# Zero-weight matmuls in the gaps of a recurrent scan on TensorE

## The reference

```python
def step(h, xt):                       # one step of the scan, h is [8,128]
    cell_inputs = jnp.concatenate([xt, h], axis=-1)
    m = cell_inputs @ weight + bias
    g_act = m[:, :units]
    c_act = m[:, units:]
    c = jnp.tanh(c_act)
    g = jax.nn.sigmoid(g_act + 1.0)
    h_new = g * h + (1.0 - g) * c
    return (h_new, h_new)
...
x = x + _L0_cond_ref(x, cond_1024, L0_cond_weight, L0_cond_bias)
x = x + _L1_cond_ref(x, cond_1024[:, None, :], ...)   # the block: norms, q/k/v, 16 heads of 8, FF 512
```

## Time and profile before

| | |
|---|---|
| median of 3 runs | 536.1 us (534.92 to 538.26) |
| the profiled execution's span | 539.5 us |
| TensorE matmul busy | 419.0 us (78%) |
| TensorE weight loads busy | 267.0 us (49%) |
| VectorE busy | 317.5 us (59%) |
| ScalarE busy | 225.6 us (42%) |
| GpSimd busy | 155.8 us (29%) |
| mean granted TensorE clock, by the profile | 0.826 |

### The profile page before, as it was taken

One profiled execution on the slowest core, in us unless ns is written; L12 is line 12 of the kernel. 1 busy time (PEld: TensorE's weight loads), 2 busy tenths in 40 slices (PEclk: granted clock), 3 DMA queues, 4 the chain that ended last, 5 costly groups with the idle time before them and its releaser, 6 DMA issues.

```text
span 539.5 us, 14126 instructions
## 1 busy us (share of the span) xinstructions
PE 419.0 (78%) x5187; PEld 267.0 (49%) x5187; DVE 317.5 (59%) x1827; ACT 225.6 (42%) x996; POOL 155.8 (29%) x343
## 2 busy tenths in 40 slices
PE   2988897876669685899998995869999999974040
PEld 1647655555457474566575653532333354353040
DVE  5444445758857678757577644660116356688864
ACT  1233223243432342454544554365465645734230
POOL 5000000224701218201417105420021423558542
PEclk9999999999999999999999999755565555565555
DMA  6109000000000000000000000000000000000000
GB/s 172 35 11 213 18 1 2 2 2 2 2 2 2 2 1 2 3 2 2 2 2 2 2 2 2 2 1 2 1 1 1 2 2 1 16 6 13 7 20 19
DMA packets 8010, 7.88 MB, mean 15 GB/s; under 512 B 1203, under 2 KB 6589, under 8 KB 7942
## 3 DMA queue, kind: packets, MB, share of 16 engines
q1 hardware_dynamic: 7846, 6.72, 5.4%
q0 software_dynamic: 96, 0.26, 0.2%
HBM read 5.91 MB, written 1.07 MB: 13 GB/s over the span
## 4 chain that ended last, share of the span: by engine, by line
PE 61%; DVE 19%; ACT 10%; POOL 5%; issue 4%; DMA 1%; SPq 0%; DVEq 0%; POOLq 0%; ACTq 0%
PE zb L686 17%; PE zb L836 7%; PE tb L637 5%; PE zb L858 5%; PE tb L779 5%; PE firsts L858 5%; DVE prod_hi L1223 4%; ACT state L993 3%; PE zb L665 3%; PE firsts L836 3%; DVE prod_lo L1229 2%; ACT state L996 2%; PE zb L671 2%; PE firsts L686 1%; PE firsts L637 1%
## 5 line engine op out<-in xcount | busy, mean ns | idle before, releaser
L686 PE MATMUL zb<-prod_hi,whh 128*128 128x8 f16 x1920 | 90.9, 171 | 42.4 <-DVE prod_hi L1223 41.3
L686 PEld LDWEIGHTS zb<-prod_hi,whh 128*128 128x128 f16 x1920 | 73.6, 106 | 96.1 <-DVE prod_hi L1223 88.2
L993 ACT ACTIVATE state<-zb 128x8 f32<-128x8 f32 x240 | 42.4, 177 | 170.4 <-PE zb L686 170.4
L1223 DVE SCALAR_TENSOR_TENSOR prod_hi<-state 128x16 f16<-128x16 f32 x255 | 47.4, 186 | 99.3 <-ACT state L996 95.1
L686 PE MATMUL zb<-prod_lo,whh 128*128 128x8 f16 x960 | 63.7, 172 | 3.0 <-DVE prod_lo L1229 1.2
L1105 ACT ACTIVATE pr<-zb 128x256 f32<-128x256 f32 x96 | 42.9, 455 | 40.9 <-PE zb L858 39.9
L1229 DVE TENSOR_TENSOR prod_lo<-prod,prod_hi 128x16 f16<-128x16 f32 x255 | 50.3, 197 | 8.7
L501 POOL TENSOR_TENSOR stat<-mv 128x4 f32<-128x4 f32 x8 | 1.6, 201 | 167.0 <-DVE mv L1310 160.0
L686 PEld LDWEIGHTS zb<-prod_lo,whh 128*128 128x128 f16 x960 | 44.4, 107 | 6.6 <-DVE prod_lo L1229 3.8
L836 PE MATMUL zb<-pr,V 128*18 128x256 f32 (+1 forms) x512 | 46.6, 457 | 0.7 <-ACT pr L1105 0.7
L858 PE MATMUL zb<-QT,KT 32*128 32x256 f16 (+1 forms) x320 | 43.4, 264 | 1.4 <-ACT pr L1105 1.4
(11 more groups left out here) (288 smaller groups left out, 744.4 us busy)
## 6 DMA issues: line engine op xcount, KB each, us to landing
mod<-ada_rows SPq DMA_DIRECT2D x4, 768.0 KB, 12.4
resid<-in_x_dram SPq DMA_DIRECT2D x6, 128.0 KB, 3.6
out_dram<-state SPq DMA_DIRECT2D x8, 64.0 KB, 2.1
out_dram<-early SPq DMA_DIRECT2D x8, 64.0 KB, 2.1
yy<-in_L_cond_w_ada_dram SPq DMA_DIRECT2D x1, 384.0 KB
early<-in_L_cond_weight_dram SPq DMA_DIRECT2D x2, 128.0 KB
resid<-in_x_dram POOLq DMA_DIRECT2D x2, 128.0 KB, 3.5
w<-in_L_cond_w_f_dram SPq DMA_DIRECT2D x1, 256.0 KB
```

Of the source, the lines that this page charges most:

```text
L686: i = pe.matmul(z_bank(t, k)[:, NB * (t % CH):NB * (t % CH) + NB], whh[:, half, p, k, :], src[:, NB * p:NB * p + NB], start=False, stop=Fa ...
L993: act.activation(r[:, 24:32], z_bank(t, 1)[:, k:k + NB], ACT.Tanh, scale=-1.0 / ZS)
L1223: dve.scalar_tensor_tensor(prod_hi[:, :], r[:, 16:32], 1.0, r[:, 0:16], ALU.add, ALU.mult).then_inc(hi_ready, 1)
```

## The change

TensorE gets matmuls whose weights are a tile of zeros (`zeros`, f16, set by VectorE at its program's start) and whose moving operand is the identity read repeatedly. They add zero to bank `zb[:, .., 0, :]` of the chunk that the scan is not in. Ten of them, of 512 columns each, stand between the transposes of `x` and `first_x_part`. In the scan a last worker, `filler`, puts some into each tick up to 249: 512 + 512 + 256 columns if no background worker put anything on TensorE since its last turn, and else 512 columns. To know that, the matmuls and transposes of the kernel are counted (`issued`).

```diff
+KEEP = STEPS - 6
+FULL, SHORT = (512, 512, 256), (512,)
...
+        zeros = sb("zeros", [P, P], F16)
...
+            def matmul(dst, left, right, **flags):
+                issued[0] += 1
+                return pe.matmul(dst, left, right, **flags)
+
+            def keep_busy(bank, sizes, first=False):
+
+                for n in sizes:
+                    pe.matmul(bank[:, 0:n], zeros[:, :], view(identh[:, 0:1], [0, n // P], [1, P]),
+                              start=first, stop=True, skip_group_check=True)
...
             x_transposes(0)
+            pe.wait_ge(consts16, 1)
+            pe.wait_ge(zeros_set, 1)
+            keep_busy(zb[:, 1, 0, :], (512,) * 10, True)
             pe.wait_ge(x_split, 1)
             pe.wait_ge(xT_sb, 1)
             first_x_part()
...
-            run(step, [prepare, tokens, attention, *tails])
+
+            def filler(now):
+                before = issued[0]
+                while now[0] < KEEP:
+                    own = issued[0] - before - 12
+                    keep_busy(zb[:, 1 - now[0] // CH % 2, 0, :], SHORT if own else FULL)
+                    before = issued[0]
+                    yield
+
+            run(step, [prepare, tokens, attention, *tails, filler])
...
+            dve.memset(zeros[:, :], 0.0).then_inc(zeros_set, 1)
             dve.memset(ones[:, :], 1.0)
```

More of the change, by code:

```diff
@@ L652, in first_x_part @@
                 for k in range(2):
-                    pe.matmul(z_bank(0, k)[:, 0:n], w0s[:, k, :], xT[:, 0:n], start=True, stop=False,
+                    matmul(z_bank(0, k)[:, 0:n], w0s[:, k, :], xT[:, 0:n], start=True, stop=False,
                               skip_group_check=True)
                     for half in range(2):
-                        pe.matmul(z_bank(0, k)[:, 0:n], b0h[:, half, k, :], onesh[:, 0:n],
+                        matmul(z_bank(0, k)[:, 0:n], b0h[:, half, k, :], onesh[:, 0:n],
                                   start=False, stop=False, skip_group_check=True)
@@ L664, in x_part @@
                             pe.wait_ge(xT_sb, c + 1)
-                        pe.matmul(zb[:, c % 2, k, 128 * q:128 * q + 128], w0s[:, k, :],
+                        matmul(zb[:, c % 2, k, 128 * q:128 * q + 128], w0s[:, k, :],
                                   xT[:, 512 * c + 128 * q:512 * c + 128 * q + 128],
@@ L670, in x_part @@
                     for half in range(2):
-                        pe.matmul(zb[:, c % 2, k, :], b0h[:, half, k, :], onesh[:, :],
+                        matmul(zb[:, c % 2, k, :], b0h[:, half, k, :], onesh[:, :],
                                   start=False, stop=False, skip_group_check=True)
@@ L685, in z_part @@
                 for p in range(2):
-                    i = pe.matmul(z_bank(t, k)[:, NB * (t % CH):NB * (t % CH) + NB],
+                    i = matmul(z_bank(t, k)[:, NB * (t % CH):NB * (t % CH) + NB],
                                   whh[:, half, p, k, :], src[:, NB * p:NB * p + NB],
@@ L707, in prepare @@
                         cols = slice(384 * h + 128 * q, 384 * h + 128 * q + 128)
-                        pe.matmul(tb[0:NB, h, 128 * q:128 * q + 128], condT[:, :], wada_s[:, cols],
+                        matmul(tb[0:NB, h, 128 * q:128 * q + 128], condT[:, :], wada_s[:, cols],
                                   start=(q == 0), stop=False, skip_group_check=True)
-                        i = pe.matmul(tb[0:NB, h, 128 * q:128 * q + 128], ones[:, 0:NB],
+                        i = matmul(tb[0:NB, h, 128 * q:128 * q + 128], ones[:, 0:NB],
                                       badar[:, cols], start=False, stop=True,
@@ L733, in prepare @@
                 for k in range(4):
-                    i = pe.matmul(ob[0:1, 0:2 * D + 1], ffw[:, k, 2 * D:2 * D + 1], ffw[:, k, :],
+                    i = matmul(ob[0:1, 0:2 * D + 1], ffw[:, k, 2 * D:2 * D + 1], ffw[:, k, :],
                                   start=(k == 0), stop=(k == 3))
@@ L739, in prepare @@
                 pe.wait_ge(gw_sb, 1)
-                pe.matmul(sbk[:, 0:D + 1], ones[:, :], gwrow[:, :], start=True, stop=True)\
+                matmul(sbk[:, 0:D + 1], ones[:, :], gwrow[:, :], start=True, stop=True)\
                     .then_inc(beta_ps, 1)
@@ L857, in scores @@
                         q = q_cols(QT[rows, b // 2, hg, :], b, chunks)
-                        ins = pe.matmul(bank[:, nq * n:nq * n + nq], KT[rows, hg, b, kb, :], q,
+                        ins = matmul(bank[:, nq * n:nq * n + nq], KT[rows, hg, b, kb, :], q,
                                         start=(n == 0), stop=(n == len(hgs) - 1),
@@ L906, in products @@
                         for c in range(NC):
-                            ins = pe.matmul(b[:, D * c:D * c + D], left[:, c, :], right,
+                            ins = matmul(b[:, D * c:D * c + D], left[:, c, :], right,
                                             start=(c == 0), stop=True, skip_group_check=True)
@@ L937, in work @@
                     for half in range(2):
-                        pe.matmul(b, onesh[:, 0:P], boh[:, half].rearrange("p c d -> p (c d)"),
+                        matmul(b, onesh[:, 0:P], boh[:, half].rearrange("p c d -> p (c d)"),
                                   start=(half == 0), stop=False, skip_group_check=True)
                     for c in range(NC):
-                        ins = pe.matmul(b[:, D * c:D * c + D], T_OT[j][:, c, :], wo_s[:, :], start=False,
+                        ins = matmul(b[:, D * c:D * c + D], T_OT[j][:, c, :], wo_s[:, :], start=False,
                                         stop=True, skip_group_check=True)
```

11 lines of the change are left out of this document (7 added, 4 removed).

## The result

| | before | changed |
|---|---|---|
| median of 4 runs each | 537.2 us (534.9 to 538.3) | 557.6 us (554.2 to 561.7) |
| the profiled execution's span | 539.5 us | 555.4 us |
| first to last `gate` of the scan | 302.0 us | 322.3 us |
| from the last `gate` to the end | 223.9 us | 219.9 us |
| TensorE matmul busy | 419.0 us | 478.9 us |

The ratio is 1.036, with an interval of 1.030 to 1.043. A run's time is its span and 1.8 us, so the profiled execution of the changed kernel, 557.2, is a median one, while that of before, 541.3, lay above these four runs of it (534.3 to 542.3 us beside the experiments). Executions over 1.5% above the fastest of the same kernel are left out of them, although nothing shows that they were disturbed.

The account below looks back on a forecast made before the run. Matmul latency, the ScalarE/VectorE loop and in some steps TensorE's issue were taken to set the scan, at 1.2 GHz. Start +9, attention +14, middle −8 gave +15 us: 554.5 on the profiled span, less 3.4, 551 us; range 523 to 575.

Parts of the forecast that it names:

- Partly held: Likeliest case, scan: steps 0 to 24 cold, 155 middle warm, 180 to 249 cold; +15 us, 551 us; chance 0.42.
- Held throughout: Rival, whole scan: once up, the clock stays at 2.4 GHz; −13 us, 523 to 528 us; chance 0.30.
- never: Rival, whole scan: zero weights don't count as work, the clock never rises; +66 us, 602; chance 0.05.
- held after a cold start: Rival, scan: first 25 steps cold at +9 us, then 225 warm; −2 us, 534 us; chance 0.13.
- oscillating: Rival, scan: filled steps raise the clock, idle TensorE loses it, about a quarter warm; +43 us, 580; chance 0.10.
- The prices at 1.2 GHz: Cold scan steps: +0.41 us without other work, +0.30 with `x_part`, +0.43 with modulation rows, +0.2 in attention.
- The gain at 2.4 GHz: Warm scan steps: 0.03 us each; six with four f32 matmuls from 1.46 to about 1.15 us.
- the 155 middle steps: Scan steps between the start and step 180: warm, −155 × 0.03 − 3 = −8 us.
- The start and attention terms: Steps 0 to about 24 cold, +9 us; steps 180 to 249 cold, 70 × 0.2 = +14 us.
- Everything behind the scan as before: After the scan: the remaining 224 us have none of the added matmuls and stay as before.
- The ten matmuls: Ahead of step 0: 4.27 us at 1.2 GHz, ending at about 11.1, cost nothing to 0.2 us.
- The missing clock record: Before's trace until 337 us: recorded full clock is a missing record; the scan runs at 1.2 GHz.

Follow-up runs that it names:

- kernels 2 to 6: Changed kernel; 2: one matmul ahead (558.8 us); 4: kernel 3, one ahead, none in steps 0-17 (553.1); 5: none from step 180 (547.2); 6: zero moving operand (558.2).
- kernel 3: Changed kernel with 1024 added columns instead of 512 in steps whose own matmuls use little of the array, 1280 in step 0; 554.7 us, ratio 1.018.
- 8, 9 and 11: Kernel 8: one matmul ahead, nothing in steps 0 to 17, then 128 to 1280 columns per step from a table; 540.1 us, ratio 1.004.
- kernel 9: Kernel 4 with 1280 columns ahead of the transposes in steps 65, 129 and 193, and 640 or 512 in attention; 552.0 us, ratio 1.015.
- kernel 11: Kernel 9 with columns from a table: 512 beside a stack's transposes and 640 to 1152 beside scores or values in attention; 542.2 us, ratio 1.002.
- kernel 7: Kernel 4 stopped after step 179, so added matmuls only in the middle; 539.8 us against 539.4, ratio 1.000.
- kernel 10: Kernel 9 with no added matmuls from step 180 on; 540.0 us against 539.8, ratio 1.002.
- kernel 12: Kernel 11 with 1792 columns in long quiet steps, 1664 beside long scores/values, 128 more beside qkv, 512 ahead of transposes in steps 110 and 174; 537.2 us, ratio 0.997.
- experiment 1: Changed kernel with the added matmuls over one row of the array instead of 128, same number and columns; 631.0 us, ratio 1.175.

## Why the prediction was right, and where its terms were off

**The mechanism.** "Partly held" is what happened: cold start, mostly warm middle, mostly cold attention. The likeliest case gave a span of 554.5 us; it was 555.4. "Held throughout" and "never" are excluded by the stretches, "held after a cold start" by attention. Of "oscillating" there is some: the clock rose and fell six times in the filled part, but with 148 of 250 steps at 2.4 GHz and not a quarter.

**The prices at 1.2 GHz.** The `x_part` step was put at 1.37 and takes 1.36; the modulation step at 1.89 and takes 1.89. A step without own work was put at 1.48 and takes 1.39: 0.37 us from its first `prod_hi` to the first added matmul instead of 0.41, and 1.02 from there to the next step instead of 1.07. The start came to +6.5 instead of +9, for this and because the clock rose at 44.6, four steps before step 25: the steps without `x_part` and modulation, put at +3.2, came to +1.0. In attention I put a pair of a scores and a values step at +0.08 a step, and all 70 steps at +0.2. The pair takes 1.38 and 1.40, together 2.78 against 2.52, so +0.13 a step:

```profile
261.95 0.40 PE L648 MATMUL zb<-prod_hi,whh 128*128 128x8 f16 x8
...
263.33 0.40 PE L648 MATMUL zb<-prod_hi,whh 128*128 128x8 f16 x8
...
264.73 0.40 PE L648 MATMUL zb<-prod_hi,whh 128*128 128x8 f16 x8
```

The 50 cold steps of attention cost 0.25 us each, more than my 0.2; 20 warm ones kept the part at +10.9 instead of +14.

**The gain at 2.4 GHz.** I took 0.03 us for a quiet step, from 0 to 0.05, on the view that the last `prod_lo` lands sooner. The group still takes 0.26 against 0.27 us, `prod_hi` 0.35 to 0.36 against 0.37, and 61 warm quiet steps gave 0.9 us, 0.015 each. The constant part of a matmul does not shrink with the clock, and 8 columns hold little else. The subtraction by which I had this from the earlier trace rows took for granted that 512 columns stream at one a cycle; the 8-column matmuls of the changed kernel show it by themselves (duration in ns, min/median/max, at 1.2 GHz and then at 2.4):

```profile
L648 PE MATMUL firsts<-prod_hi,whh x112: 167/168/214, 15.1 to 34.6; 128*128 128x8 f16 x112
```
```profile
L648 PE MATMUL zb<-prod_hi,whh x216: 166/166/180, 72.9 to 101.5; 128*128 128x8 f16 x108
```

The six modulation steps that I wanted to see shrink ran at 1.2 GHz. So the 155 middle steps, put at −8, came to +2.8: 32 of them were cold where I had none (+6.8 us), and the 123 warm ones gave 3.9 instead of 8. The 3 us that I gave to TensorE's long steps came out (3.1 in the 67 warm steps with own work); the quiet ones gave half of what I took. This is the term that was most off, by 10.8 us. The start and attention terms, 5.6 too high, the 4.0 us behind the scan and the 0.5 ahead of it offset it. That the span came out within 1 us is luck: the parts were less well known than the sum looks.

**Behind the scan.** "Everything behind the scan as before" was 4.0 us off. The traces show what goes with it: the time at 2.4 GHz behind the scan is 10.2 us in before's profile with 223.9 us for that part; 17.1 in the changed kernel with 219.9, and in kernels 2 to 6, 8, 9 and 11 with 219.8 to 222.9; 23.9 in kernels 7 and 10 with 218.1 and 218.3; 10.2 in kernel 12 with 225.0. No added matmul runs there, and the program is the same; where the rises fall in it shifts. Before itself does this from run to run: beside the ninth experiment its runs of 534.5 to 534.9 us had a mean clock of 0.838, those of 539.5 to 540.0 us one of 0.825 to 0.829. So the 3.4 us that I took off to come from the profiled span to the median held for before, whose profiled execution was at the upper end, and not for the changed kernel, whose profiled execution was a median one. With the 1.8 us between a span and its time that makes the 6.6 us between the 551 forecast and the 557.6 measured, with the span within 1 us.

**The ten matmuls** were put at nothing and cost nothing; they end at 10.87, `first_x_part` starts at 11.08. Overlooked was what they give: `first_x_part` runs at 2.4 GHz behind them, its first product in 0.49 us instead of 0.79, and the first `gate` comes 0.5 us earlier.

```profile
6.68 4.19 PE L653 MATMUL zb<-identh,zeros 128*128 128x512 f16 x10
11.08 0.49 PE L648 MATMUL firsts<-xT,w0s 128*128 128x128 f32 x2 [0.21 <-DVE b0h L1234]
```

**The missing clock record** was read rightly. In the changed kernel, whose record changes from 10.46 us on, the same `x_part` matmuls take 0.78 us at 15.42 with 0.50 recorded as they took in before under a recorded 1.00.

**The rival's price.** I gave "held throughout" 13 us. Kernel 12 holds the clock over 224 of 250 steps and gains 5.7 us in them, but it adds more columns (226,560 against the changed kernel's 184,064), and they have a price at 2.4 GHz too: in the 137 steps from 25 on that both kernels did at 2.4 GHz, it is 3.6 us shorter than before and the changed kernel 5.5. An estimate for a clock held with the changed kernel's own columns: for 204 of the 250 steps some kernel has the step at 2.4 GHz with the same number of columns, and their differences to before add up to −9 us. The rest are the first 18 steps and, but for a few, scores and values steps, which gave 0.02 us or less each where the changed kernel had them at 2.4 GHz. So 13 was too high, by the 0.03 us that I took for a quiet step. The case's 0.30 stood on the clock being held with these columns, and no run shows that: every kernel that added 512 columns beside scores or values lost it in attention.

The Trainium skill's page "TensorE: Matmul & The Clock Gate" (Why this matters for your kernels) advises keeping TensorE free of long idle gaps. The trace agrees in part: stretches with full columns held. It disagrees where the fill uses few rows: in the scan of experiment 1 TensorE was busy for 395.05 of 397.20 us, and no rise came.

**What stays open.** Why kernels 3, 9 and 11 vary by 13 to 18 us from run to run. Their longer executions have the lower mean clock (kernel 9: 0.759 at 543.1 us, 0.713 at 561.0), but no profile of a short and a long execution side by side was taken. Whether a fill that starts at 2.4 GHz could hold it from step 0: kernel 3, with 1280 columns in step 0 and 1024 beside the bias rows, kept it from 8.5 to 18.8 us and lost it before the modulation steps. What loses the clock in the middle: of kernel 11's falls at 140.1, 177.6 and 290.3 us kernel 12 has one, at 176.0, but which of its four edits did it was not separated, and falls move between executions of the same instructions (experiment 10).

## What to carry over

Work that is put in to hold a clock costs what of it does not fit into the gap when the clock is not held (here 0.3 to 0.4 us a step of 1.07) and gives only what the loop spends in streaming when it is (0.015 in a quiet step). More of it holds the clock longer and takes back part of the gain. Before adding it, read how much of the critical loop is streamed columns: a chain of 8-column matmuls with a constant 0.17 us each has next to nothing to gain. The gain was in the steps that TensorE's own work makes long (up to 0.5 us each), so there it may be worth trying, with all 128 rows, and ahead of a place where TensorE stands waiting, not behind it. No kernel here became faster by it: kernel 10, which fills the stands of kernel 7, measured the same as before (1.002), as kernel 7 did (1.000).

## What the runs showed of the hardware

- Zeros count: all-zero matmuls over 128 rows and 128 columns had the clock up as data does (558.2 against 557.6 us), one-row matmuls of as many columns never had it up in the scan (512 columns 602 to 630 ns throughout).
- With one-row matmuls ahead of it, the weight load of the 128-row `prod_hi` matmul came only 0.01 us ahead of that matmul, with 128-row ones 0.21: 1.59 us a step against 1.39.
- A matmul of 8 columns takes 168 ns at 1.2 GHz and 166 at 2.4, one of 512 columns 607 and 377 (medians in the changed kernel).
- A fall shows within a step or two in the very durations of narrow work: in the changed kernel the same eight values matmuls took 0.41 us at 240.54 and 0.63 at 242.65, with the record changing at 242.6.

```profile
240.54 0.41 PE L648 MATMUL firsts<-pr,V 128*18 128x128 f32 x8
...
242.65 0.63 PE L648 MATMUL firsts<-pr,V 128*18 128x128 f32 x8
```

- Where a trace has no clock change yet, the record reads 1.00 whatever the clock is: the whole scan of the one-row kernel, at 602 to 630 ns for 512 columns, is recorded at full clock. A run's mean clock has the same weakness: beside the twelfth experiment before's execution of 540.4 us has 0.585 and that of 540.2 us 0.829.
- The same program differs by 5 us from run to run, and its mean clock with it (before: 534.5 us at 0.838, 540.0 us at 0.826); in the profiles the time behind the scan goes with how much of it is granted 2.4 GHz.
- The same instructions lost 2.4 GHz in different places: at 140.4 and 171.1 us in kernel 9, at 104.0, 144.9 and 185.9 in kernel 10, which is the same up to step 179.
